# A decoder layer on one core: loop bodies unrolled and recut, two heads to 128 rows

## The reference, cut to what matters

```python
x = x + attn(layernorm(x))            # 16 heads of 16, rope, causal window of 64
x = x + xattn(layernorm(x), ctx, m)   # on the (128 x 256) block read as 128 channels x 256 positions
x = x + moe(layernorm(x))             # 8 experts, top 2 by biased sigmoid, and a shared expert

# attn:  q, k, v = x @ w_qkv.T;  q, k = rope(q), rope(k)
#        scores = q k / 4, kept where 0 <= row - col < 64;  softmax;  @ v;  @ w_out.T
# xattn: q = Wq @ target + bq, k, v = W @ source + b  (16 heads of 8, 256 x 256 scores a head)
#        dot = mask * dot - (1 - mask) * 1e6;  softmax * mask;  @ v
# moe:   scores = sigmoid(x @ gate.T); the two best by scores + bias; each expert
#        silu(r @ w1.T) * (r @ w3.T) @ w2.T with r = x * score;  + the shared expert
```

## Time and profile before

| | |
|---|---|
| runs | 481.31, 485.94, 486.96 us; median 485.94 |
| profiled execution | 484.94 us, span 483.1 us |
| PE busy | 369.4 us (76%), 2512 instructions |
| DVE busy | 292.1 us (60%), 590 |
| ACT busy | 155.0 us (32%), 300 |
| POOL busy | 91.7 us (19%), 104 |
| granted TensorE clock, mean | 0.83 of full speed |
| DMA | 40.06 MB, mean 83 GB/s |

### The profile page before, as it was taken

How to read it: one execution, slowest core, us unless ns; L and a number is a source line. 1 busy time by engine, 2 the same in 40 slices (tenths; PEclk the granted TensorE clock), 3 DMA queues, 4 the chain that set the end, 5 groups by cost and what they waited for, 6 DMA issues and landing times.

```text
span 483.1 us, 7161 instructions
## 1 busy us (share of the span) xinstructions
PE 369.4 (76%) x2512; PEld 238.2 (49%) x2512; DVE 292.1 (60%) x590; ACT 155.0 (32%) x300; POOL 91.7 (19%) x104
## 2 busy tenths in 40 slices
PE   3314841778896999769986999679869988986797
PEld 2202420524434788424444887144348862434786
DVE  2696045387545866965538678955277669505664
ACT  1200401024763041135750420256711400582222
POOL 5870001140000232320000341400003210000222
PEclk9756765666999799958997999679977995698799
DMA  8690025665033446090232563551242450021000
GB/s 325 154 150 9 25 66 142 146 93 67 9 104 105 82 135 131 24 125 11 69 102 73 119 141 76 72 60 55 86 115 22 149 112 3 0 69 66 1 12 12
DMA packets 53470, 40.06 MB, mean 83 GB/s; under 512 B 5868, under 2 KB 52660, under 8 KB 53188
## 3 DMA queue, kind: packets, MB, share of 16 engines
q1 hardware_dynamic: 51428, 39.14, 36.7%
q10 hardware_dynamic: 2016, 0.58, 0.5%
HBM read 19.40 MB, written 12.68 MB: 66 GB/s over the span
## 4 chain that ended last, share of the span: by engine, by line
PE 50%; DVE 21%; DMA 9%; ACT 7%; issue 6%; SPq 5%; POOL 1%; DVEq 0%; ACTq 0%; POOLq 0%
PE ps L707 12%; DVE max L1256 6%; PE ps L655 6%; PE ps L671 5%; PE ps L727 5%; PE ps L633 4%; PE ps L519 4%; DMA d_o<-o 2%; DMA stack_0q<-mT 2%; PE ps L719 2%; DMA o1s<-d_o 2%; SPq L385 2%; ACT prob L885 2%; PE ps L598 2%; PE ps L545 2%
## 5 line engine op out<-in xcount | busy, mean ns | idle before, releaser
L1256 DVE TENSOR_REDUCE max<-ps 128x2 f32<-128x512 f32 x128 | 80.3, 683 | 16.7 <-PE ps L633 15.4
L885 ACT ACTIVATE prob<-ps 128x512 f32<-128x512 f32 x128 | 69.5, 595 | 45.2 <-PE ps L655 44.9
L707 PE MATMUL ps<-xn1T,w_sb 128*128 128x256 f32 (+1 forms) x360 | 74.9, 356 | 3.3 <-DVE u L1288 3.3
L707 PEld LDWEIGHTS ps<-xn1T,w_sb 128*128 128x128 f32 x360 | 62.8, 207 | 10.4 <-DVE u L1288 4.1
L1024 POOL TENSOR_TENSOR rstd<-var_eps,minus_half 128x2 f32<-128x2 f32 x13 | 9.0, 693 | 277.1 <-DVE var_eps L1121 277.1
L1049 POOL TENSOR_TENSOR u_times_u<-u 128x256 f32<-128x256 f32 (+1 forms) x45 | 29.7, 660 | 66.9 <-DVE u L1288 53.3
L671 PE MATMUL ps<-prob,v 128*32 128x256 f32 x512 | 41.1, 401 | 0.9 <-ACT prob L885 0.7
L1263 DVE RECIPROCAL o2s<-o2s 128x256 f32<-128x256 f32 x8 | 14.0, 1752 | 41.5 <-DMA o2s<-d_o 41.5
L727 PE MATMUL ps<-w_sb,hT 128*128 128x256 f32 x144 | 38.1, 386 | 0.8 <-DVE hT L1298 0.3
L633 PE MATMUL ps<-stack_1k,stack_1q 96*128 96x256 bf16 x128 | 33.4, 386 | 4.1 <-DVE max L1256 3.9
L1192 DVE TENSOR_REDUCE max<-ps 128x4 f32<-128x512 f32 x32 | 21.9, 690 | 22.3 <-PE ps L549 22.1
(11 more groups left out here) (123 smaller groups left out, 537.5 us busy)
## 6 DMA issues: line engine op xcount, KB each, us to landing
d_o<-o SPq DMA_DIRECT2D x8, 512.0 KB, 2.8
stack_q<-parts SPq DMA_DIRECT2D x24, 128.0 KB, 4.3
stack_k<-parts SPq DMA_DIRECT2D x24, 128.0 KB, 5.7
d_stack<-parts SPq DMA_DIRECT2D x8, 384.0 KB, 2.7
w_sb<-in_w SPq DMA_DIRECT2D x1, 2304.0 KB, 9.8
d_o<-o SPq DMA_DIRECT2D x8, 256.0 KB, 2.3
d_stack<-parts SPq DMA_DIRECT2D x8, 256.0 KB, 2.3
stack_0q<-d_stack SPq DMA_DIRECT2D x4, 320.0 KB
```

The source lines that it names most:

```text
L707: mm = pe.matmul(ps[:, banks_of(batches).up[n % 2], D * w + cols.start:D * w + cols.stop], w13_sb[:, e, k, w, :], xn3T[:, k, cols], start= ...
L885: act.activation(prob[:, h % 8, :], ps[:, B0 + h % 2, :], ACT.Exp).then_inc(exp2, 1)
L1256: v.tensor_reduce(max2[:, a, c // 8, 2 * (c % 8):2 * (c % 8) + 2], ps[:, A_BANKS[a][c % len(A_BANKS[a])], :].rearrange("p (g s) -> p g s", ...
```

## The change

The pairs and the arithmetic stay the same, but for the layout of the cross stacks. The `Fori` loops are gone: all five bodies, from -1 to 3, are written out, and the self attention of pair 0 is body -1.

**Cross stacks.** One stack per pair parity (`stack2[i % 2]`) holds both sequences, and two heads lie in the 128 rows: one in rows 0 to 63, one in rows 64 to 127. Row r of a half is slot r mod 8 of depth r div 8: six slots for the parts, two for the mask terms and the maximum (`MASK_SLOTS`, `MAX_ROW2`). A group is two heads: four matmuls of 64 rows into two PSUM banks, one VectorE maximum over both banks (128 x 1024), one exponential over both. The maximum rows come in two DMAs. The key stack and the mask rows of pair i+1 are written during body i's first stage, the query stack and the self stack of pair i+2 at the end of body i. Nothing goes through DRAM on the way to a stack.

**Order of a body.** First nine turns, one for each expert of pair i-1, with the 16 groups of cross maxima of pair i (`WIDE`), the context projections and the eight self maxima of pair i+1 (`SELF_A`) spread over them; the self maxima use one bank (`MISC`), two where there is no cross attention. Then the exponentials: the first sequence's eight cross groups with the eight self chunks three steps later, and then the second sequence's. Then the output projection of the self attention, turn and projections of pair i+2, the query projection of pair i+1, and the preparation and first two up projections of experts i.

**Gates.** They are transposed to 8 rows, copied, stored to DRAM and loaded back to all partitions in four broadcast DMAs (`gate_rows`).

**Smaller.** The residual is kept in `xr`, with no copy by ScalarE; the scaled mask is made by GpSimd; the mask rows are made ahead of the first ropes, and GpSimd's fills wait for them; x and masks are loaded a pair further ahead; the experts' weights are loaded in three pieces in body 0; `prob1` holds two self chunks.

In the diff's core the five `body` functions are, in this order, those of SP, TensorE, ScalarE, GpSimd and VectorE; `j` is the self attention's pair and `f` the experts'.

```diff
+WIDE = ((0, 1, 2), (3, 4), (5, 6), (7, 8), (9, 10), (11, 12), (13,), (14,), (15,))
+SELF_A = ((), (), (0,), (1,), (2,), (3, 4), (5, 6), (7,), ())
+TURN_A0, TURN_SELF = 4, 8
+SELF_LAG = 3
...
+def cross_part(i, n, c):
+    sp.wait_ge((high2, mid2, parts2_ready)[c][n], i + 1)
+    for slot in HOLDS[n][c]:
+        sp.dma_start(stack2[i % 2][n][slot::STEP2].rearrange("r u a t -> r (u a t)"),
+                     parts2[:, c].rearrange("p a t -> p (a t)")).then_inc((q2_ld, k2_ld)[n][i % 2], 16)
...
+def gate_rows(turn, batches=BOTH):
+    cols = columns(batches)
+    sp.wait_ge(gT_sb, turn + 1)
+    sp.dma_start(d_gates[:, cols], gT[:, cols]).then_inc(g_st, 16)
+    sp.wait_ge(g_st, 16 * (turn + 1))
+    for q in range(E // 2):
+        rows = d_gates[2 * q:2 * q + 2, cols].rearrange("(o e) t -> o e t", o=1)
+        sp.dma_start(g_bc[:, 2 * q:2 * q + 2, cols],
+                     rows.broadcast_to([P, 2, cols.stop - cols.start])).then_inc(g_ld[q], 16)
...
+def body(i, has_cross, has_experts, has_self, has_next):
+    j = i + 1
     if has_self:
+        if i > 0:
+            sp.wait_ge(scores_b2, 16 * i)
+        if i == -1:
+            sp.wait_ge(mrow_st, 16 * 16)
+        cross_mask_rows(j)
+        for c in range(3):
+            cross_part(j, 1, c)
+        if has_next:
+            sp.wait_ge(v2_proj, j + 1)
+            load_ctx(j + 1)
+    if i == 0:
+        for e in range(0, E + 1, 3):
+            load_experts(e, e + 3)
+    if has_cross:
+        cross_max(i, 0)
     if has_self:
+        self_max(j)
+    if has_cross:
+        cross_max(i, 1)
     if has_experts:
         store(i - 1)
     if has_self:
+        self_out_store(j, 0)
+        self_out_load(j, 0)
+        self_out_store(j, 1)
+    if has_cross:
+        cross_out_store(i, 0)
     if has_self:
+        self_out_load(j, 1)
+    if has_cross:
+        cross_out_load(i, 0)
+        cross_out_store(i, 1)
+        cross_out_load(i, 1)
     if has_self:
+        for c in range(3):
+            cross_part(j, 0, c)
+    if has_next:
+        for c in range(3):
+            self_part(j + 1, c)
+    if i + 3 < PAIRS:
+        sp.wait_ge(x1_ready, j + 1)
+        load_x(i + 3)
+    if has_cross and has_self:
+        if has_next:
+            sp.wait_ge(x2_ready, 2 * i + 2)
+            load_masks(i + 2)
+        gate_rows(i)
...
+def cross_max_scores(i, g):
+    a, u, p = g // U, g % U, i % 2
+    if g == 0:
+        pe.wait_ge(k2_ld[p], N_STACK2 * (i // 2 + 1))
+        pe.wait_ge(mask2_ld[p], N_MASK2 * (i // 2 + 1))
+        pe.wait_ge(q2_ld[p], N_STACK2 * (i // 2 + 1))
+        if i == 0:
+            pe.wait_ge(exp1, 8)
+    if g < 2:
+        wait(pe, exp2, 16 * i - 1 + g if i else 0)
+    else:
+        pe.wait_ge(max2_done, 16 * i + g - 1)
+    for t in range(2):
+        for half in range(2):
+            rows = slice(HALF * half, HALF * (half + 1))
+            mm = pe.matmul(ps[:, GROUPS[g % 2] + half, D * t:D * (t + 1)],
+                           stack2[p][0][rows, u, a, P * t:P * (t + 1)],
+                           stack2[p][1][rows, u, a, :], start=True, stop=True)
+    mm.then_inc(scores_a2, 1)
...
+def cross_exp_scores(i, a, u):
+    n, p = U * a + u, i % 2
+    if u == 0:
+        pe.wait_ge(mrow2_ld[a], 32 * (i + 1))
+    if n < 2:
+        pe.wait_ge(max2_done, 16 * i + 15 + n)
+    else:
+        pe.wait_ge(exp2, 16 * i + n - 1)
+    for t in range(2):
+        for half in range(2):
+            rows = slice(HALF * half, HALF * (half + 1))
+            mm = pe.matmul(ps[:, GROUPS[u % 2] + half, D * t:D * (t + 1)],
+                           stack2[p][1][rows, u, a, P * t:P * (t + 1)],
+                           stack2[p][0][rows, u, a, :], start=True, stop=True)
+    mm.then_inc(scores_b2, 1)
...
+def experts_gates(i, batches=BOTH):
+    pe.wait_ge(gates_ready, i + 1)
+    if batches == BOTH:
+        pe.wait_ge(exp1, 8 * (i + 2))
+        wait(pe, v1_ready, i + 3 if i + 2 < PAIRS else 0)
+    elif batches == SECOND:
+        pe.wait_ge(gT_sb, i)
+    for a in range(batches.start, batches.stop):
+        mm = pe.transpose(ps[0:E, banks_of(batches).gates, P * a:P * (a + 1)], gates[:, a, :], id_f[:])
     mm.then_inc(g_ps, 1)
...
+def body(i, has_cross, has_experts, has_self, has_next):
+    j, f = i + 1, i - 1
+    banks = (MISC,) if has_cross else (MISC, 0)
+    for k in range(E + 1):
+        if has_cross:
+            for g in WIDE[k][:-1]:
+                cross_max_scores(i, g)
+        if has_experts and k + 2 <= E:
+            expert_up(f, k + 2)
+        if has_self and k == 0:
+            cross_project_keys(j)
+        if has_self and k == 1:
+            cross_project_values(j)
+        if has_self:
+            for c in SELF_A[k][:1]:
+                if c == 3 and has_cross:
+                    pe.wait_ge(mT2_sb, 2 * i + 1)
+                self_max_scores(j, c, banks)
+        if has_cross:
+            cross_max_scores(i, WIDE[k][-1])
+        if has_self:
+            for c in SELF_A[k][1:]:
+                self_max_scores(j, c, banks)
+        if has_cross and k == TURN_A0:
+            if has_self:
+                pe.wait_ge(max1_done, 8 * j + 3)
+            else:
+                pe.wait_ge(gT_sb, i)
+            cross_turn_max(i, 0)
+        if has_self and k == TURN_SELF:
+            self_turn_max(j)
         if has_experts:
+            expert_down(f, k)
+    if has_cross:
         if has_self:
+            pe.wait_ge(mT1_sb, j + 1)
+        else:
+            pe.wait_ge(mT2_sb, 2 * i + 1)
+        cross_turn_max(i, 1)
+    for step in range(U + 2 + SELF_LAG - 1 if has_self else U + 2):
+        if has_cross and step < U:
+            cross_exp_scores(i, 0, step)
+        if has_self and 0 <= step - SELF_LAG + 1 < 8:
+            self_exp_scores(j, step - SELF_LAG + 1, banks)
+        if has_cross and 2 <= step < U + 2:
+            cross_values(i, 0, (step - 2) // 2, step % 2)
+        if has_self and 0 <= step - SELF_LAG < 8:
+            self_values(j, step - SELF_LAG)
+    if has_cross:
+        for step in range(U + 2):
+            if step < U:
+                cross_exp_scores(i, 1, step)
+            if step >= 2:
+                cross_values(i, 1, (step - 2) // 2, step % 2)
     if has_self:
         for a in range(2):
             self_project_out(j, a)
+    if has_next:
+        self_turn(j + 1)
+        self_project(j + 1, 0)
+    if has_self:
+        cross_project(j)
+    if has_next:
+        self_project(j + 1, 1)
+        self_project_v(j + 1)
+    if has_cross and has_self:
+        experts_prepare(i)
+        experts_begin(i)
...
+def exponential(i, a, u):
+    n = U * a + u
+    act.wait_ge(scores_b2, 16 * i + n + 1)
+    if n % 2 == 0:
+        wait(act, values2, 8 * i + n // 2 - 1)
+    bank = GROUPS[u % 2]
+    act.activation(prob[:, 2 * (u % 4):2 * (u % 4) + 2, :], ps[:, bank:bank + 2, :], ACT.Exp).then_inc(exp2, 1)
...
+def body(i, has_cross, has_experts, has_self, has_next):
     j, f = i + 1, i - 1
+    banks = (MISC,) if has_cross else (MISC, 0)
+    for k in range(E + 1):
+        if has_experts:
+            tanh_up(f, k)
+        if has_self and k == 1:
+            cross_high(j, 1)
+        if has_self and k == 3:
+            cross_mid(j, 1)
+        if has_cross and k == TURN_A0:
+            turn_max(i, 0)
+        if has_self and k == TURN_SELF:
+            self_turn_max(j)
+    if has_cross:
+        turn_max(i, 1)
+    for step in range(U + SELF_LAG if has_self else U):
+        if has_cross and step < U:
+            exponential(i, 0, step)
+        c = step - SELF_LAG + 1
+        if has_self and 0 <= c < 8:
+            self_exponential(j, c, banks)
+            if c == 5:
+                self_out(j, 0)
+    if has_cross:
+        cross_out(i, 0)
     if has_self:
+        self_out(j, 1)
+    if has_cross:
+        for u in range(U):
+            exponential(i, 1, u)
+        cross_out(i, 1)
+    if has_next:
+        self_tokens(j + 1)
     if has_self:
+        cross_high(j, 0)
+        cross_mid(j, 0)
+    if has_next:
+        self_values_copy(j + 1)
+        self_high(j + 1)
+        self_mid(j + 1)
+    if has_cross and has_self:
         experts_tokens(i)
         experts_logits(i)
+        experts_gates(i)
...
+def body(i, has_cross, has_experts, has_self, has_next):
     j, f = i + 1, i - 1
     if has_experts:
+        for k in range(E + 1):
+            expert_product(f, k)
+    if has_next:
+        inverse_deviation(0, j + 1)
     if has_self:
+        cross_mask_scale(j)
+        inverse_deviation(1, j)
+    if has_next:
+        self_sine(j + 1)
+        pool.wait_ge(high1, j + 2)
+        pool.wait_ge(rope_done, 2 * j + 4)
+        nc.gpsimd.tensor_tensor(qk1[:], qk1[:], parts1[:, 0], ALU.subtract).then_inc(rest1_ready, 1)
+    if has_cross and has_self:
+        inverse_deviation(2, i)
+    if has_next:
+        pool.wait_ge(mid1, j + 2)
+        pool.wait_ge(rest1_ready, j + 2)
```

(59 more changed lines are left out.)

959 lines of the change are left out of this document (379 added, 580 removed).

## The result

The changed kernel takes 521.41 us (median of 4 runs, 518.82 to 524.61) where the kernel before took 483.62 on the same chip (478.06 to 486.96): ratio **1.083, 95% interval 1.077 to 1.089**. It is slower, as forecast, but three times as much as the 2.5% of the forecast. (Ratios here are taken over undisturbed runs alone, so they are not always the quotient of the medians shown.) The profiled execution took 524.61 us, span 522.8; it is the longest of the four, 3.2 us over their median, and that much of its excess may be its own.

What follows compares the result with a forecast made beforehand. A row of stages with different limits bounds the kernel, 101.5 us a body. First scores at 82, 174.5, 284.5, 391, values' end 449, plus tail: span 497.5, time 498 us; own range 484 to 512, whole range 463 to 522.

Steps and rivals of the forecast that it cites:

- A: Stage of experts and maxima: 50 us at 5.5 a turn, 31.5 in body 0, 38.6 in body 3.
- B1: Exponentials of first cross batch and self, until the last self exponential: 15 us, 16 in body 0, steps of 1.75.
- T: A body's last self exponential, from which times in C are counted; residual forecast at T+19.
- C: From the last self exponential to the next body's first scores: 45 us, 41.5 in body 2.
- step 4: Stage C as a serial chain on VectorE's queue: residual T+19, query projection T+24.3, experts' norm T+37, first scores T+45.
- step 5: Gates through DRAM: hidden in A, exposed in the tail's second turn, first turn covered by early norm: +2.5 on 45.8.
- step 1: Up to body 0's first cross scores: 82 us instead of 99.0, first self maximum at 32.5, residual at 65.5.
- the two doubts: In B1, whether 64-row matmuls pair and whether tiling-mode changes drain: no pairing with full drains adds some 5 us.
- The engines do not wait for each other: Faster rival: A costs VectorE's 41 us, C runs at full clock with shorter DMA trips: 458 us; chance 0.29.
- The clock stays low in A: Slower rival: half clock adds 2.2 us to seven turns, 15 a body in three bodies: 543 us; chance 0.12.
- The pairing doesn't pair: Rival in B1: 0.25 x 8 more where TensorE bounds, some 5 us, 503 us; inside the forecast, no separate chance.

Runs made afterwards that it cites:

- e4: The changed kernel with TensorE's idle time in C filled with matmuls into a bank nothing reads: 508.47 us, ratio 1.056 to the kernel before.
- e3: The changed kernel with GpSimd's two subtractions of the self parts cut to a quarter of their columns: 514.64 us, ratio 1.052 to the kernel before.
- e2: The changed kernel with second cross output and experts' norm moved ahead in the queues of C: 511.44 us, ratio 1.060 to the kernel before.
- e1: The changed kernel without the gates' trip through DRAM, gating left out of the result: 512.75 us, ratio 1.063 to the kernel before.
- e6: The changed kernel with up projections put behind the self scores and last wide scores in TensorE's queue: 499.93 us, ratio 1.023 to the kernel before.
- the combined kernel: The changed kernel with the edits of e2 and e6, last turns' gates spread by TensorE, and earlier mask loads: 476.84 us, ratio 0.990 to the kernel before.
- e5: The changed kernel with both heads of each cross group read from rows 0 to 63, so no pairing: 555.98 us, ratio 1.141 to the kernel before.

## Why the prediction was wrong

The sign was right, and most steps: two-bank maxima (1.22 for 1.2), the pitch of A (5.3 to 6.1 for 5.5), steps of 1.66 to 1.68 us in B1 with paired matmuls once the clock is high (1.75 forecast), the residual at T+18.9, the loss sitting in C. The size was off, 1.083 for 1.025, by 25 us of span, and about half of it is one term. The 521.41 us lie beyond the forecast's own 484 to 512 and at the upper edge of its whole range, 463 to 522. (The sum itself ends a little low: a span of 497.5 and the 1.8 around it are 499.3, not 498.)

**C, step 4 of the forecast: +13 us.** This is the step that failed, by its size: the chain was right link by link, the links were too short. In body 1: the query's projection ended at T+25.9 for T+24.3, since the self projection took 3.78 at the low clock where I had taken 2.5 between the two levels; the last split at T+32.5 for T+31; the experts' norm at T+41.1 for T+37, 2.7 of these 4.1 us being the two instructions held by GpSimd, which no step priced (the kernel before has the same subtractions, but in its stage of maxima, not beside the second cross output and the norm); the first wide maximum at T+51.5 for T+45, the up projections having taken 6.21 us at a granted clock of 0.62. The experiments put 2.9, 3.6 and 5.5 us on the clock (e4) and 3.0 and 2.6 on GpSimd (e3), with the excess 4.0, 6.5 and 2.5: clock and sharing are enough for it in bodies 0 and 1, though each was taken away alone and never both. In body 2, without subtractions, it is the clock: the up projections alone took 6.73 us there and 3.70 in e4. The experiments also show what I had missed by arguing for a "series": 9 us of C were only the order in VectorE's queue (e2).

**Tail, step 5: +4.5.** "In the first turn the norm is done early and takes the trip's place" failed. VectorE idles 4.76 us there, then does the second cross output and norm, and they are late in turn; the trip takes 7.2 us, not 6.1. Both turns pay, 8.4 us of idle time in all, where I gave 2.5 net. Nor was the trip hidden in all of A: body 3's first gated read waited 1.03 us for it.

**Start, step 1: +4.0.** The step from the residual to the first scores was right: 69.29 to 86.02 is 16.7 for 16.5. The residual came 3.8 us later than the 65.5 worked out. The first self maximum stood at 34.56, not 32.5; the other 1.7 us lie between it and the residual. No run isolates them, so this stays open.

**B1: +3.1.** Of the two doubts the pairing came out: 0.33 us a group, seam included. The drain at a change of tiling mode, for which the Trainium skill's rule ("TensorEngine Tiling (Array Packing)", Tiling Modes, Key Properties) stood, is there too, and small, about 0.1 us (the line of 248.62 above): the 64-row group and the 99-row scores, each with another mode behind, take 0.33 and 0.32 us from start to start, the full-width mask, with none, 0.22. One more seam a step makes some 0.8 us in the eight steps of a B1, an estimate from these rows, where the 5 us of the prediction were for full drains and no pairing. What is over is that the first steps run at the low clock: 0.50 from 232 to 236 us, 0.98 behind it.

**A: -0.4,** right by its own working, with bodies 1 and 2 3.0 under the forecast and body 3 2.4 over it (the wait for the gates' rows and the low clock behind it, e1). But the forecast took the loop as given by the change; it was one line's place in TensorE's queue, worth 8.6 us a body (e6).

**The rivals.** "The engines do not wait for each other" was wrong for this kernel, as the gap between 48.3 us and e6's 39.7 shows; it describes what a reordering makes of it: the combined kernel's 476.84 lies 19 us above its 458. "The clock stays low in A" was wrong where experts run, 0.98, and true of body 0's A, 0.55, which waits for VectorE anyway. "The pairing doesn't pair" was wrong, and so was its price: 5 us, where taking it away cost 28 by the ratios, because I let the granted clock stand.

## What to carry to other kernels

When work of several stages is merged, write down each engine's queue as a loop and ask of every instruction that waits what stands behind it and does not need it: here two such places, the up projections ahead of the self scores and the second cross output behind the ropes, held over 20 us each (of the second, 12 came back as waits in A until SyncE's order was changed too). A stage that is shortened uncovers the transfers it hid, so the issue order of the DMA queue has to be looked at in the same step. Price a serial stretch with TensorE at its low level, and VectorE's instructions with two SBUF inputs and its normalising ones up to the end of the GpSimd instruction that lies beside them.

## What the runs showed of the hardware

- Some VectorE instructions beside a GpSimd subtraction wait for its end: a product of two SBUF tiles took 1.26 us for 0.43, two normalising ones 2.60 for 0.73. With smaller GpSimd instructions they took 0.42 and 1.15. A reciprocal beside the same subtraction kept its 1.74.
- Two 64-row matmuls in different halves of the rows run side by side: a group of four took 0.39 us, 0.61 with both heads read from one half, both at the high clock (A of the changed kernel and of e5).
- A change of tiling mode, from 64 rows to full or from full to column quarters, cost about 0.1 us at the high clock.
- One after the other, matmuls that fill half of the rows left the granted clock at 0.52 to 0.54 with TensorE busy 94% of the stage (e5); in pairs it was 0.82 to 0.87 with TensorE busy 85%.
- A filling of 7.93 us at the high clock was lost again after 4.04 us of idle time (e4, bodies 0 and 1: 0.50 in the transposes of body 1). The one that lasted until the transposes, in body 2, left the up projections at 1.00.
